# Two GNN layers on one core: where the norm of each later group's first slot is put, and when it is split and set up

## The reference

```python
# layer 0
h = jnp.maximum(_layernorm(x, axis=-1), 0.0)
x = x + (jnp.einsum('nm,bmo->bno', adj, h @ weight) + bias)
# layer 1: 5 steps of a gated unit, both matrices are adj
h = jnp.maximum(_layernorm(x, axis=-1), 0.0)
def step(h, _):
    m = jnp.einsum('nm,bmd->bnd', adj, h)
    av = jnp.concatenate([m, m], axis=-1)
    u3 = h @ u3_w.T + u3_b
    z = jax.nn.sigmoid(av @ w3_w.T + w3_b + u3)
    r = jax.nn.sigmoid(av @ w4_w.T + w4_b + u3)
    hv = jnp.tanh(av @ w5_w.T + w5_b + (r * h @ u5_w.T + u5_b))
    return (1.0 - z) * h + z * hv, None
x = x + jax.lax.scan(step, h, None, length=5)[0]
```

## Time and profile before

| | us |
|---|---|
| median of 3 runs | 1546.14 (1543.82 to 1546.3) |
| the profiled execution | 1547.53, its span 1545.7 |
| TensorE busy | 1459.4 (94%) |
| VectorE busy | 1254.6 (81%) |
| ScalarE busy | 947.4 (61%) |

### The profile page before, as it was taken

How to read it: one execution, slowest core, us unless ns; L and a number is a source line. 1 busy time by engine, 2 the same in 40 slices (tenths; PEclk the granted TensorE clock), 3 DMA queues, 4 the chain that set the end, 5 groups by cost and what they waited for, 6 DMA issues and landing times.

```text
span 1545.7 us, 19917 instructions
## 1 busy us (share of the span) xinstructions
PE 1459.4 (94%) x6951; PEld 672.2 (43%) x6951; DVE 1254.6 (81%) x1697; ACT 947.4 (61%) x1470; POOL 172.6 (11%) x388
## 2 busy tenths in 40 slices
PE   4778999999999899999999999999999989999997
PEld 3433444444443344444444334444444434444443
DVE  8866888788877978888877778888887887887777
ACT  5535566776647665676565755676664766566653
POOL 1312004040200000340011000403021000000000
PEclk9889999999999999999999999999999999999998
DMA  4010333422223242433122233342222323233322
GB/s 180 1 28 19 84 58 64 93 52 48 49 55 56 55 92 52 109 63 68 33 51 55 55 79 61 66 116 52 45 49 58 56 60 60 52 82 68 66 50 80
DMA packets 316626, 97.42 MB, mean 63 GB/s; under 512 B 310256, under 2 KB 311152, under 8 KB 316528
## 3 DMA queue, kind: packets, MB, share of 16 engines
q1 hardware_dynamic: 314800, 95.49, 29.3%
...
q10 hardware_dynamic: 1728, 0.66, 0.2%
...
## 4 chain that ended last, share of the span: by engine, by line
PE 76%; DVE 13%; ACT 5%; issue 4%; POOL 1%; DMA 1%; ACTq 0%; SPq 0%; DVEq 0%; POOLq 0%
PE ps_a L569 27%; PE ps_c L569 13%; PE ps_b L569 6%; PE ps_u L625 6%; PE ps_u L629 6%; PE ps_u L627 6%; PE ps_v L627 4%; PE ps_v L629 4%; PE ps_v L625 4%; DVE nx_lo L1197 2%; ACT ysc L817 1%; DVE rh L1243 1%; DVE rh L1239 1%; DVE t_lo L1118 1%; ACT nx_hi L833 1%
## 5 line engine op out<-in xcount | busy, mean ns | idle before, releaser
L569 PE MATMUL ps_a<-t_hi,nx_hi 128*128 128x512 f16 x640 | 245.1, 383 | 21.5 <-DVE m_lo L1233 9.0
L569 PE MATMUL ps_a<-t_lo,nx_hi 128*128 128x512 f16 x640 | 245.1, 383 | 0.0
L569 PE MATMUL ps_a<-t_hi,nx_lo 128*128 128x512 f16 x640 | 244.7, 382 | 0.0
L872 ACT ACTIVATE rh<-ps_v,bias,w_inv 128x512 f32<-128x512 f32 x160 | 124.0, 777 | 92.9 <-PE ps_v L629 92.9
L859 ACT ACTIVATE rh<-ps_a 128x512 f32<-128x512 f32 x144 | 84.9, 590 | 146.1 <-PE ps_a L569 117.7
L868 ACT ACTIVATE m_hi<-rh 128x512 f16<-128x512 f32 x144 | 90.1, 628 | 126.2 <-DVE rh L1228 125.5
L1278 DVE TENSOR_TENSOR rh<-rh,area 128x512 f32<-128x512 f32 x160 | 109.1, 691 | 68.3 <-ACT rh L877 64.5
L1233 DVE SCALAR_TENSOR_TENSOR m_lo<-rh,m_hi 128x512 f16<-128x512 f32 x144 | 98.8, 690 | 47.8 <-ACT m_hi L868 42.5
L877 ACT ACTIVATE rh<-ps_u,bias,w_inv 128x512 f32<-128x512 f32 x160 | 120.2, 774 | 22.2 <-PE ps_u L629 20.8
L625 PE MATMUL ps_u<-m_hi,w_hi 128*128 128x512 f16 x320 | 121.9, 381 | 12.1 <-DVE m_lo L1233 12.1
L885 ACT ACTIVATE area<-ps_u,bias,w_inv 128x512 f32<-128x512 f32 x160 | 122.3, 771 | 17.2 <-PE ps_u L629 16.9
...
## 6 DMA issues: line engine op xcount, KB each, us to landing
...
nx_hi<-s SPq DMA_TRANSPOSE x128, 2.4
nx_lo<-s SPq DMA_TRANSPOSE x128, 2.5
...
nx_hi<-h_hi SPq DMA_TRANSPOSE x96, 2.4
nx_lo<-h_lo SPq DMA_TRANSPOSE x96, 2.5
```

The lines of the kernel that those rows point to most:

```text
L569: last = nc.tensor.matmul(o[:, :], a[:, PLACE[k], j, :], b[:, k, j, :], start=(opens and j == 0 and n == 0), stop=(j == HB - 1 and n == 2) ...
L872: nc.scalar.activation(cand[:, q, :], V_BANK[q][:, :], ACT.Tanh, bias=bias[:, BV:BV + 1], scale=w_inv[:, CAND:CAND + 1]).then_inc(cand_rea ...
```

## The change

For the first slot of groups 1 to 3 (`in_ny`), layer 1's norm is written to `ny`, which layer 0's second slot has been read from, instead of `nx`, and the first step's product reads it there. It no longer waits for the last step's blocks, so all four parts and the sums stand in the last step, two of them in its first half; `turn_first` and `first_h` of that slot stand there too. In the first step, slot 1's norm (still in `nx`) moves forward: half of `normalise` ahead of the candidates of quarters 2 and 1, parts 0 to 2 within the step, part 3 in the second step. `turn_end` of the group's slot 1, which overwrites part of `ny`, waits for the first step's B1. Group 0 keeps its order but for one `round_n` that is asked for three operations sooner.

```diff
+        def in_ny(p, slot):
+            return slot == 0 and p > 0
...
@@ n_place_free
             elif layer == 1 and slot == 0 and p > 0:
+                e.wait_ge(prod_done, max(made(g_layer(p, 1), k, LAYER_ORDER) for k in ks))
+            elif layer == 1 and slot == 1 and p > 0:
                 e.wait_ge(prod_done, max(made(g_step(p - 1, END, 1), k) for k in ks))
@@ SP turn_end, slot 1
-                    sp.wait_ge(prod_done, KS * (g_layer(p + 1, 1) + 1))
+                    sp.wait_ge(prod_done, made(g_step(p + 1, 0, 0), K_B1))
+                    for k in range(2):
+                        sp.wait_ge(first_in[0][k], 4 * 16 * (p + 2))
@@ SP step
                     store(p - 1, 0)
-                    turn_first(p, 0)
                     turn_end(p - 1, 1)
...
                 if t == END and slot == 1:
                     if final(p):
                         turn_end(p, 0)
+                    else:
+                        turn_first(p + 1, 0)
@@ ACT step, candidates
+                    if first0:
+                        normalise(p, 1, 1, range(2))
+                    if first1 and p == 0:
+                        round_n(0, 1, 1, 2)
                     if first1:
-                        round_n(p, 1, 1, 2)
+                        round_n(p, 1, 1, 3)
                     candidate(s - 1, 2)
...
-                    if t == 0:
-                        round_n(p, 1, slot, 3)
                     if first0:
-                        normalise(p, 1, 1, range(1))
+                        normalise(p, 1, 1, range(2, 3))
...
                     if first0:
-                        normalise(p, 1, 1, range(1, 3))
+                        round_n(p, 1, 1, 0)
+                        normalise(p, 1, 1, range(3, 4))
@@ DVE step
+                if steps_ahead(p, t, slot, END, 1):
+                    sum_n(p + 1, 1, 0, [0])
...
                 rest_m(g, 3)
+                if steps_ahead(p, t, slot, END, 1):
+                    sum_n(p + 1, 1, 0, [1])
...
                 if steps_ahead(p, t, slot, END, 1):
-                    sum_n(p + 1, 1, 0, [1])
-                    rest_n(p + 1, 1, 0, 2)
+                    first_h(p + 1, 0)
```

More of the change, by code:

```diff
@@ L440, in turn_first @@
                 for q in range(4):
-                    for done, source, dest in ((n_hi_done[1], nx_hi, h16_hi[slot]),
-                                               (n_lo_done[1], nx_lo, h16_lo[slot])):
+                    for done, source, dest in ((n_hi_done[1], ny_hi if in_ny(p, slot) else nx_hi, h16_hi[slot]),
+                                               (n_lo_done[1], ny_lo if in_ny(p, slot) else nx_lo, h16_lo[slot])):
                         sp.wait_ge(done, 4 * n + 1 + q // 2)
@@ L620, in step_product @@
                     pe.wait_ge(turned_lo[k], 16 * (e + 1))
-                block_product(k, nx_hi, nx_lo)
+                if t == 0 and in_ny(p, slot):
+                    block_product(k, ny_hi, ny_lo)
+                else:
+                    block_product(k, nx_hi, nx_lo)
             def product(bank_out, w, a_hi, a_lo, q, start=True, stop=True, reopen=False):
@@ L821, in round_n @@
             def round_n(p, layer, slot, part):
-                n, dest = n_layer(p, slot), (ny_hi, nx_hi)[layer]
+                n, dest = n_layer(p, slot), nx_hi if layer == 1 and not in_ny(p, slot) else ny_hi
                 rows4 = ysc[:, :, :].rearrange("p (q b) d -> p q (b d)", q=4)
@@ L1006, in step @@
                         round_n(p + 1, 0, 1, 1)
+                    if t == END and slot == 1:
+                        round_n(p + 1, 1, 0, 1)
                     evacuate(g, s, 1)
@@ L1009, in step @@
                 round_m(g, 0)
+                round_m(g, 3)
                 if first0 and p > 0:
-                    normalise(p, 1, 1, range(3, 4))
-                round_m(g, 3)
+                    round_n(p, 1, 1, 1)
                 if steps_ahead(p, t, slot, END, 1):
-                    round_n(p + 1, 1, 0, 0)
+                    round_n(p + 1, 1, 0, 2)
                 if steps_ahead(p, t, slot, 3, 0):
@@ L1018, in step @@
                 round_m(g, 2)
-                if first0 and p > 0:
-                    round_n(p, 1, 1, 0)
                 sigmoid_r(s, 0)
@@ L1033, in step @@
                     normalise(p, 1, 1, range(2, 4))
-                if first0 and p > 0:
-                    round_n(p, 1, 1, 1)
                 sigmoid_z(s, 3)
@@ L1044, in step @@
                     round_n(p + 1, 0, 1, 2)
-                if steps_ahead(p, t, slot, END, 1):
-                    round_n(p + 1, 1, 0, 2)
+                if first0 and p > 0:
+                    round_n(p, 1, 1, 2)
                 sigmoid_z(s, 2)
@@ L1188, in rest_n @@
             def rest_n(p, layer, slot, part):
-                n, hi, lo = n_layer(p, slot), (ny_hi, nx_hi)[layer], (ny_lo, nx_lo)[layer]
+                n, hi, lo = n_layer(p, slot), *((nx_hi, nx_lo) if layer == 1 and not in_ny(p, slot) else (ny_hi, ny_lo))
                 rows4 = ysc[:, :, :].rearrange("p (q b) d -> p q (b d)", q=4)
@@ L1384, in step @@
                     e = n_sum(before_p, before_t, other)
-                    if first1:
-                        rest_n(p, 1, 1, 2)
+                    if first1 and p == 0:
+                        rest_n(0, 1, 1, 2)
                     new_state(s - 1, other, 0)
                     new_state(s - 1, other, 1)
-                    if t == 0:
-                        rest_n(p, 1, slot, 3)
+                    if first1:
+                        rest_n(p, 1, 1, 3)
                     if sums:
@@ L1409, in step @@
                                 output(p, 0, high, batch)
+                        rest_n(p + 1, 1, 0, 1)
                     layer_sum(*before)
@@ L1413, in step @@
                         rest_n(p + 1, 0, 1, 1)
-                if t == 0:
+                if first0 and p > 0:
+                    rest_n(p, 1, 1, 0)
+                elif t == 0:
                     first_h(p, slot)
                 sum_m(g, 0)
+                if steps_ahead(p, t, slot, END, 1):
+                    sum_n(p + 1, 1, 0, [0])
                 if sums:
@@ L1425, in step @@
                     sum_n(p + 1, 0, 1, [0])
+                if steps_ahead(p, t, slot, END, 1):
+                    sum_n(p + 1, 1, 0, [1])
+                if first0 and p > 0:
+                    rest_n(p, 1, 1, 1)
                 rest_m(g, 2)
```

24 lines of the change are left out of this document (12 added, 12 removed).

## The result

The changed kernel takes 1534.2 us (median of 4 runs, 1533.81 to 1534.43), the kernel before 1546.22 (4 runs, 1543.82 to 1548.97). The ratio is 0.9916, with a 95% interval of 0.9897 to 0.9934: 12.0 us faster. The forecast was 1535.

What follows compares the result with a forecast made beforehand. TensorE, busy 94% of the span, bounds the kernel, so only its idle time can be won. 1547.53 - 11.3 = 1536.2 for the profiled execution, 1.4 above the median, so 1535; range 1530 to 1541.5.

Steps and rivals of the forecast that it cites:

- The last step's start and the sums: Last step, ScalarE and VectorE: start costs nothing; `round_n` of part 2 waits for sums, new idle of 1.6 us before u1.
- The first step: First step: `evacuate` for S3 at 489.7 instead of 492.77, S3 without a wait at 491.6: 1.8 us early.
- S3 to u1: First step, S3 to u1: the old wait of 0.85 kept (0.75 by laying out), so 1.9 us early.
- The second step: Second step: part 2 done before, so side 1 starts 3.3 us early, r3 at 533.5; gain 3.3 us a boundary.
- The waits before r0 and r3: Second step: about 1.0 and 1.8 us remain in place of 1.65 and 1.69, with low clock behind them kept.
- SP: SP's queue: slot 1's transposes landed at 523.9, wanted at 526.3 and 526.1: 2.2 us to spare, no cost.
- that rival: Slot 1's transposes on SP come too late: at 2.0 us each, 5.7 lost a boundary, 1564; chance 0.05.
- The sum: Three boundaries of 3.3 us make 9.9; 1.4 more at the second boundary, where S3's gap and low clock go: 11.3.
- What can be had: TensorE's idle time in first and second steps: 8.3 us at each of three boundaries, 25 us, 1.6% of the time.
- The first rival: Low clock behind the last step's new wait at each boundary: 5.1 us lost of 11.3, 1540; chance 0.20.
- The second: Low clock behind r0 and r3 of the second step goes at all three boundaries: 5.1 us more, 1530; chance 0.08.
- The gaps only move: Last step's chain is held 3 to 5 us, first step starts late: 1543 to 1548, no difference; chance 0.10.

Runs made afterwards that it cites:

- e1: Changed kernel, but in the last step ScalarE's `round_n` of part 2 stands behind the sigmoids of r0 and r3, part 3 behind r2's: 1528.32 us.
- e7: Edits of e1 and e5 together, plus VectorE's `rest_n` of part 2 and half 0 of slot 1's sums behind `rest_m` of quarter 1: 1517.37 us.
- x4: Changed kernel, but the eight `normalise` ahead of candidates 2 and 1 in the first step stand behind the state's first rounding: 1536.93 us.
- x1: Changed kernel, but the first slot's first state (transposes and two VectorE additions) is set up in the first step again: 1537.77 us.
- y1: Kernel before, with only the norm's destination changed, its needed waits and reading places; every engine's order kept: 1544.24 us.
- x2: Changed kernel, but part 2 of slot 1's norm is split in the second step again, ahead of `new_state` and candidate 2: 1544.32 us.
- e5: Changed kernel, but `first_h` of every slot 1 stands behind `rest_m` of quarter 3 on VectorE in the second step: 1525.69 us.
- the repeat: The changed kernel once more, unedited: 1532.96 us (one run).

## Why the prediction was right, step by step

- **The last step's start and the sums.** Half 1's first operation over at 466.05 by the prediction, at 465.94 in the trace; `round_n` 466.1 and 465.98, `m_hi` 467.05 and 466.95, the sigmoid 467.55 and 467.42. u1 was to be 1.6 late and is 1.55 late; with the 0.26 that stood there before, the idle time is 1.80 (1.64 in the bracket). e1 shows that the place of `round_n` makes 1.0 of it, e7 that the place of VectorE's `rest_n` makes the other 0.6, which the prediction did not tell apart.
- **The first step.** Candidate 1 over by 484.68 where side 1 was to start at 484.85; side 1 over at 488.53, not 488.7; `evacuate` at 489.53, not 489.7; S3 without a wait at 491.48, not 491.6. x4 shows 0.75 lost when `normalise` stands behind the candidates, x1 0.46 when the state is set up in the first step. That `new_state` is hardly earlier (0.2), but fewer things stand between it and S3, was the right reading; the prediction did not say that the longest of them was ScalarE's wait of 2.66 for slot 0's last part. This is the largest piece of the gain. It is read from rows: y1 shows that the new place does not remove it by itself, and no run puts slot 0's parts alone back into the first step.
- **S3 to u1.** I laid out 0.75 and kept the old 0.85; 0.58 was measured. The laying out was the better number and should have been used. This is a mis-sized term, 0.2 to 0.3 us at each boundary.
- **The second step.** Side 1 at 516.8 by the prediction, 516.55 in the trace; `first_h` 526.3 and 526.10; r3 533.5 and 533.26. x2 shows the mechanism and gives it 1.3.
- **The waits before r0 and r3.** The prediction has 1.0 and 1.8, with the 0.16 that brackets leave out; measured were 0.98 and 1.53, with it 1.14 and 1.69. e5 shows what they hung on: the place of `first_h`.
- **SP.** Spare 2.2 by the prediction, 3.8 in the trace. I counted sixteen pitches and two landings, but a landing counts from its transpose's issue (507.25 to 509.86, 519.76 to 522.32: 2.6 each), so it takes a pitch's place: 14 pitches. As nothing waits there, no number of the sum changed. (The price of that rival, at 2.0 a transpose, is 11 less 5.5, 5.5 a boundary and not 5.7.)
- **The sum.** 3.3 a boundary, 3.5 measured. 11.3 in all, 13.5 between the two profiled executions: 3 x 0.2, and some 1.6 for the low clock behind r3 at the second boundary, which was to stay. Between the medians it is 12.0, because the profiled execution of before lay 1.3 above its median and that of the changed kernel 0.2 below. That 1535 and 1534.2 lie 0.8 apart is therefore partly luck; the terms were off by 2.2.
- **What can be had.** The prediction put it at 25 us, all of TensorE's idle time in the first and second steps. It left out the 1.49 in layer 0's last round, three times, and the pair before r0 and r3 in group 0, of which e5 took 1.4.
- **The clock.** The first rival, low clock behind the new wait, did not come in any of the three places, nor in x1 to x4, e5 or the repeat. The second came at one boundary of three. There the argument was weak: I tied "the low clock stays" to "the idle is hardly shorter". In the nine profiled executions here with waits before r0 and r3 of 0.6 to 1.5 and 1.5, low clock followed at 20 of 27 boundaries; in the three with 0.40 before r3 and 0.71 before u1, at none of 9. In group 0 the same pair (1.49 and 1.53) stood in ten executions and low clock followed in one (x2). So with the same waits it varies from one execution to the next, and from place to place. The forecast should have counted the low clock behind r3 as a share of the 5.1 us and not as all or nothing.
- **The gaps only move** did not happen: each step that was to be earlier is.

The Trainium skill (TensorE: Matmul & The Clock Gate, Part 1) says that the low clock is the default and that activity releases it. The traces agree in that each low stretch at a boundary stands behind idle time and none came without. By these runs the length of the waits alone does not decide it: e1 has 0.98 and 1.52 without one.
